# A recurrent transformer kernel on one core: runs written out, the key swap ahead of the feed-forward's wait, and 87 of 361 stages at other steps

## The chip, the cores and the metric

The kernel runs on one core of one Trainium2 chip. A time is the device time of one execution in microseconds. The kernel before takes 2809.85 us, the median of three runs (2808.43 to 2814.73). Durations in this document come from one execution that was also profiled and took 2810.37 us.

The names of the engines in the rows are PE (TensorE, matrix multiply; PEld is its weight load), ACT (ScalarE), DVE (VectorE), POOL (GpSimd) and SP (SyncE, which here only issues transfers; SPq is its queue).

## The reference

```python
for l in range(6):                                   # layers; x is (4, 128, 128)
    x = attention(x, None, ..., causal=True, bias, freqs) + x      # self: 16 heads, one shared key/value head of 64
    x = attention(x, context, ..., causal=False) + x               # cross: context is (4, 2048, 128)
    x = feedforward(x, ...) + x                                    # 128 -> 2*512 gated -> 128
out = layernorm(x, final_g, stable=True) @ proj_w
# attention: layernorm, q = xn@wq, k,v = kv@wkv, one learned null key/value in front,
#            l2norm of q and k, softmax(q k^T + bias), @ v, @ wo, layernorm
# then: x = x + out;  x = x + small 16-head causal attention(layernorm(x));
#       x = x + gated recurrent scan over the batch rows, and a tanh output, of layernorm(x)
```

The bulk is cross attention: for each of 24 pairs of layer and batch row, 16 heads of 128 queries against 2048 keys.

## The kernel before

One **run** is one pair of layer and batch row, n = 0 to 23 (`n // 4` is the layer). The work of a run is in three parts. The **front** (stages whose name begins with `f_`) is self attention, the cross query, and keys and values of the context. The **core** is cross attention. The **back** (`b_`) is the output projection and the feed-forward. Stages of the core outside its tile steps are `e_`; `s_` is setup; `t0_`, `t1_`, `u_`, `v_` are the final tail for batch rows 0, 1, 2 and 3.

The core is cut into 64 tiles (4 groups of 4 heads, 16 blocks of 128 keys), each 128 keys by 512 query columns. A tile is: two float16 score matmuls into one of three PSUM banks `psS` (L1050); ACT takes the exponent twice, once rounded to the matmul's format as `PH` (L885) and once exact as `P` (L888); DVE subtracts, `PL = P - PH` (L634); PE multiplies values with `PH` twice (L1098, L1099) and with `PL` once (L1101), into `psO`. There are 4 buffers for `P` and 8 for `PH` and `PL`. PE runs the value matmuls of a tile 6 steps behind its scores (AHEAD), DVE the subtraction one step behind.

A **window** is 65 steps (one for the null key, then 64 tiles). In one window PE, ACT, DVE and POOL each work on the core of run n, on the front of run n + 1 and on the back of run n - 1. Each engine has a table, PLAN_PE and so on, that names which stages it executes behind its part of step s. An engine executes its instructions in this order and waits at semaphores; nothing else sets the order. So a stage that stands early in an engine's table and waits for another engine holds up every tile step behind it.

Windows 1 to 22 are in a hardware loop of 11 iterations with two windows each (`Fori`, L321); window 0, window 23 and the last one, without a core, are written out. SP has a queue of its own with a loop over layers (L383): `context` loads the context of a run, `swap` (L377, L378) copies the two halves of the keys `KT` onto each other's partitions, and `query_weights`, `front_weights`, `back_weights` load the weights of a layer. The back weights of a layer may be overwritten only when the feed-forward of the last run of the layer before is done (`ff_w2`). PE begins a window by waiting for the swap of that run (`kv_swap`).

Stages that matter below: on PE `f_turn_q_sa` (L1043, turns the self-attention queries), `b_turn` (L1035 on `psA`, turns the normalised row of the back), `f_sk2` (L1050 on `psL`), `f_wo` (L1155 on `psL`), `b_down` (L1213). On DVE `f_unit_sa` (L576), `f_null` (L650 to L652), `f_V3` (L684, L686), `b_out` (L707 and the layernorm behind it, to L491 on `back_xn`), `b_end` (L721). On ACT `f_hi_sa` (L894, L895); on POOL `f_low_sa` (L461 on `qs_all`), `f_klow` (L461 on `ks`) and `f_rot` (L452 to L455).

Of the kernel before, what the change touches and what calls it, by code (L numbers as in the profile page):

```python
# [20 lines left out]
L, B, N, D = 6, 4, 128, 128  # L21
# [11 lines left out]
RUNS = L * B  # L33
# [29 lines left out]
def build(nc, x, ctxT, wpack, gcols, gout, null_k, null_v, tail_w, tail_cols, bo, emb,  # L63
          c_pack, out):
    with ExitStack() as ctx:
# [176 lines left out]
        def at(s, core, back):  # L242
# [8 lines left out]
            0: ["s_bias"], 4: ["f_turn_sa"], 5: ["f_proj_sa", "f_proj_sa2", "f_kv0"], 7: ["f_kv1"], 8: ["u_turn_fin"],  # L251
# [14 lines left out]
            4: ["f_raw_sa", "f_raw_sa2"], 7: ["f_kraw0"], 8: ["f_sq_sa"], 10: ["f_kraw1", "s_table"],  # L266
            13: ["f_hi_sa", "f_kraw2"], 14: ["f_kraw3"], 15: ["f_ksq"], 17: ["f_QT_sa"], 20: ["b_tanh"],
# [3 lines left out]
            41: ["t1_back0"], 45: ["t1_back2"], 52: ["f_raw_ca"], 53: ["f_sq_ca"], 54: ["f_KT"], 59: ["f_hi_ca"],  # L271
            62: ["f_QT_ca"], 65: ["v_gates2", "v_exp0", "v_exp1", "v_exp2", "v_exp3", "v_back0", "v_back2", "v_gates3"],
        }
        PLAN_DVE = {
            0: ["f_begin", "f_norm_sa"], 1: ["e_null", "s_bias", "f_xnT_sa"], 2: ["s_null"], 3: ["b_spread3"],
            4: ["b_invert3"], 5: ["b_widen3"], 6: ["f_V0", "f_V1"], 7: ["b_scale3", "t0_largest", "u_largest"],
            9: ["f_ss_sa", "t0_final", "u_final"], 10: ["s_turned", "s_table"], 11: ["f_V2", "f_unit_sa", "t0_in"],
# [16 lines left out]
            61: ["t1_z"], 64: ["b_end", "u_z"],  # L294
# [3 lines left out]
            0: ["f_sa", "s_null"], 1: ["f_rot"], 6: ["f_sa_q"], 7: ["f_low_sa", "t0_fin", "u_fin", "s_mask"], 11: ["t0_y"],  # L298
            12: ["u_y", "t0_y2", "b_out"], 13: ["b_ff", "f_kv"], 14: ["u_y2"], 16: ["t1_fin"], 19: ["f_klow"], 20: ["t1_y"],
            21: ["t1_y2"], 30: ["f_out"], 37: ["f_ca"], 38: ["s_rows"], 40: ["f_ca_q"], 49: ["f_low_ca"], 54: ["t0_z"],  # L300
            56: ["t1_z"], 60: ["u_z"], 65: ["v_fin", "v_y", "v_y2", "v_z"],
        }

        def drive(eng, plan, stages, core_step=None):
# [16 lines left out]
            with eng.Fori(0, (RUNS - 2) // 2) as k:  # L321
                window((k * 2 + 1, 1), (k * 2, 0), (k * 2 + 2, 0))
                window((k * 2 + 2, 0), (k * 2 + 1, 1), (k * 2 + 3, 1))
# [8 lines left out]
        def _(sp):  # L332
# [50 lines left out]
            with sp.Fori(1, L) as l:  # L383
                context(l * B)
                swap(l * B - 1, 1)
                sp.wait_ge(sem("ca_proj"), l * B * 2)
                query_weights(l)
                front_weights(l)
                context(l * B + 1)
                swap(l * B, 0)  # L390
                context(l * B + 2)
                sp.wait_ge(sem("ff_w2"), l * B)
                back_weights(l)
                swap(l * B + 1, 1)
                context(l * B + 3)
                swap(l * B + 2, 0)
# [1004 lines left out]
```

## Time and profile before

| | |
|---|---|
| median of three runs | 2809.85 us |
| the profiled execution | 2810.37 us, its span from first to last instruction 2808.6 us |
| PE busy | 2519.6 us, 90% |
| DVE busy | 2314.1 us, 82% |
| ACT busy | 2057.7 us, 73% |
| POOL busy | 613.8 us, 22% |
| mean granted clock of TensorE | 0.971 of full |
| first window's first instruction of the core | 97.80 us |
| windows 1 to 22 (the loop) | 197.04 to 2586.13 us |

A busy share is the time in which at least one instruction of the engine is under way. In square brackets behind a row of the timeline stands how long the engine had been idle before that instruction and what released it; "issue" there means that the profile shows nothing that it waited for. DMA transfers are of this kind.

### The profile page before, as it was taken

The page shows a single profiled execution, that of the slowest core. Times are in us where ns is not written, and L with a number is a line of the kernel's source. Part 1 is how long each engine was busy: PE and PEld are TensorE (multiplying, and loading weights), DVE is VectorE, ACT ScalarE, POOL GpSimd, SP SyncE. Part 2 cuts the span into 40 slices and gives each one's busy share as a digit, 9 for nine tenths or more (in the row PEclk, how much of TensorE's full clock was granted, in tenths as well). Part 3 has the DMA queues.
Part 4 walks back from the last instruction along what each step waited for, and adds up shares of the span by engine and source line. Part 5 has one row for each costly group of instructions (what it writes and reads, how often), then busy time and mean ns, then how long its engine had stood idle before and what let it go on. Part 6 is the DMA issues. An engine that isn't in the chain of part 4 may idle for free.

```text
span 2808.6 us, 44144 instructions
## 1 busy us (share of the span) xinstructions
PE 2519.6 (90%) x12652; PEld 1529.2 (54%) x12652; DVE 2314.1 (82%) x4427; ACT 2057.7 (73%) x3861; POOL 613.8 (22%) x392
## 2 busy tenths in 40 slices
PE   4799999989999998999998999998999999999776
PEld 2455555555555555555555555555555555555455
DVE  6688889888888887888887887887888887888876
ACT  2677877777877877778777877877787787788541
POOL 2312312312212213123123123122132131230000
PEclk7899999999999999999999999999999999999986
DMA  3000010000000001001001001001001001000000
GB/s 120 23 8 16 24 34 16 23 29 16 23 31 20 24 1 44 9 16 49 9 16 44 8 16 49 8 16 44 4 21 39 12 23 29 16 9 24 1 1 4
DMA packets 16661, 64.43 MB, mean 23 GB/s; under 512 B 2241, under 2 KB 7410, under 8 KB 11642
## 3 DMA queue, kind: packets, MB, share of 16 engines
q1 hardware_dynamic: 16378, 61.13, 6.8%
q8 instruction: 120, 1.97, 0.3%
q14 instruction: 163, 1.34, 0.1%
HBM read 48.25 MB, written 0.29 MB: 17 GB/s over the span
## 4 chain that ended last, share of the span: by engine, by line
DVE 32%; PE 28%; issue 21%; POOL 10%; ACT 7%; DMA 2%; DVEq 1%; SPq 0%; ACTq 0%; POOLq 0%
DVE PL L634 11%; POOL rn L420 7%; PE psS L1050 6%; PE psO L1098 4%; PE psO L1101 4%; PE psO L1099 4%; DVE rows_sb L613 3%; ACT P L888 3%; DVE rows_sb L605 3%; DVE oTs L618 2%; ACT PH L885 2%; DVE ss L568 2%; PE psL L1155 2%; POOL qs_all L461 2%; PE psL L1162 2%
## 5 line engine op out<-in xcount | busy, mean ns | idle before, releaser
L634 DVE TENSOR_TENSOR PL<-P,PH 128x512 fp32r<-128x512 f32 x1536 | 1126.4, 761 | 121.9 <-ACT P L888 67.9
L885 ACT ACTIVATE PH<-psS 128x512 fp32r<-128x512 f32 x1536 | 955.4, 622 | 155.7 <-PE psS L1050 134.2
L888 ACT ACTIVATE P<-psS 128x512 f32<-128x512 f32 x1536 | 964.2, 628 | 72.8 <-DVE PL L634 72.6
L1050 PE MATMUL psS<-QT,KT 128*128 128x512 f16 x3072 | 926.1, 385 | 0.8 <-ACT P L888 0.7
L1098 PE MATMUL psO<-PH,V 128*128 128x512 f32 x1536 | 880.7, 573 | 0.0
L1101 PE MATMUL psO<-PL,V 128*128 128x512 f32 x1536 | 608.3, 396 | 0.0
L1099 PE MATMUL psO<-PH,VL 128*64 128x512 f32 x1536 | 607.1, 395 | 0.0
L1050 PEld LDWEIGHTS psS<-QT,KT 128*128 128x128 f16 x3072 | 215.1, 99 | 339.5 <-issue 247.0
L1098 PEld LDWEIGHTS psO<-PH,V 128*128 128x128 f32 x1536 | 293.5, 191 | 181.3 <-issue 8.8
L1101 PEld LDWEIGHTS psO<-PL,V 128*128 128x128 f32 x1536 | 289.7, 189 | 154.1 <-issue 2.6
L420 POOL TENSOR_TENSOR rn<-ssc,neghalf 128x16 f32<-128x16 f32 (+2 forms) x73 | 235.6, 3228 | 354.2 <-DVE ssc L569 302.2
L420 POOL TENSOR_TENSOR front_rstd<-front_ve,neghalf 128x1 f32<-128x1 f32 x80 | 43.1, 539 | 1119.0 <-DVE front_ve L489 1119.0
L1099 PEld LDWEIGHTS psO<-PH,VL 128*64 128x64 f32 x1536 | 211.3, 138 | 41.6
L936 ACT ACTIVATE Ps<-psL 128x512 f32<-128x512 f32 x96 | 57.3, 597 | 154.2 <-PE psL L1050 154.2
L461 POOL TENSOR_TENSOR qs_all<-qsq,qs_all 128x1088 f16<-128x1088 f32 (+1 forms) x48 | 116.5, 2427 | 134.4 <-ACT qs_all L895 134.4
L613 DVE STREAM_TRANSPOSE rows_sb<-rcol 64x512 f32<-64x512 f32 x192 | 133.5, 704 | 5.3
L1176 PEld LDWEIGHTS psL<-W,ctx_sb 128*128 128x128 f32 x768 | 99.4, 192 | 23.3 <-ACT qraw L907 14.4
L1043 PE MATMUL psL<-ident,qs_all 128*128 128x128 f16 x768 | 52.2, 222 | 66.4 <-POOL qs_all L461 66.4
L907 ACT ACTIVATE qraw<-psL 128x512 f32<-128x512 f32 x96 | 57.3, 597 | 71.8 <-PE psL L1162 51.8
L1176 PE MATMUL psL<-W,ctx_sb 128*128 128x128 f32 x768 | 104.2, 279 | 1.1 <-ACT kraw L950 1.1
L1144 PE MATMUL psL<-Ps,Vs 128*128 128x512 f32 x192 | 101.5, 611 | 3.4 <-DVE Ps L670 3.4
L461 POOL TENSOR_TENSOR ks<-ksq,ks 128x1024 f16<-128x1024 f32 x24 | 58.6, 2441 | 204.2 <-ACT ks L960 204.2
(365 smaller groups left out, 2844.2 us busy)
## 6 DMA issues: line engine op xcount, KB each, us to landing
ctx_sb<-ctxT SPq DMA_DIRECT2D x24, 1024.0 KB, 4.8
KT<-KT SPq DMA_DIRECT2D x48, 256.0 KB, 3.7
W<-wpack SPq DMA_DIRECT2D x6, 1280.0 KB, 6.3
W<-wpack SPq DMA_DIRECT2D x6, 1088.0 KB, 7.0
W<-wpack SPq DMA_DIRECT2D x6, 576.0 KB, 5.2
KT<-biasM SPq DMA_DIRECT2D x1, 1024.0 KB
W<-tail_w SPq DMA_DIRECT2D x1, 832.0 KB
P<-biasW SPq DMA_DIRECT2D x1, 512.0 KB
```

The costliest lines, as they stand in the source:

```text
L420: nc.gpsimd.tensor_tensor(out_, in_, neghalf[0:out_.shape[0], 0:width], ALU.pow).then_inc(sem(done), 1)
L461: nc.gpsimd.tensor_tensor(half, whole, high, ALU.subtract).then_inc(sem(tag + "_lo"), 1)
L613: nc_v.transpose(rr, rc.unsqueeze(2).broadcast_to([64, QCOL // 32, 32])).then_inc(sem(tag + "_row"), 1)
L634: nc_v.tensor_tensor(PL[:, here, :], P[:, t % PSLOTS, :], PH[:, here, :], ALU.subtract).then_inc(sem("p_lo"), 1)
L885: nc_a.activation(PH[:, t % HSLOTS, :], bank, ACT.Exp, scale=SIM_SCALE).then_inc(sem("p_hi"), 1)
L888: nc_a.activation(P[:, t % PSLOTS, :], bank, ACT.Exp, scale=SIM_SCALE).then_inc(sem("ca_exp"), 1)
L1050: ins = mm(bank, keys[part], q, start=(part == 0), stop=(part == 1))
L1098: mm(bank, V[:, par, j, :], PH[:, here, :], start=False, stop=False)
L1099: mm(bank[0:DH, :], VL[:, par, j, :], PH[:, here, :], start=False, stop=False)
L1101: mm(bank, V[:, par, j, :], PL[:, here, :], start=False, stop=(j == KT_N - 1)).then_inc(sem("ca_pv"), 1)
L1144: mm(psL[:, g % 2, :], Vs[:], Ps[:, g % 2, :], start=True, stop=False)
L1176: ins = mm(psL[:, t % 2, a * 128:(a + 1) * 128], ctx_sb[:, k * 128:(k + 1) * 128], weights(W_CAKV, W_CAKV + 128), start=True, stop=True)
```

## The change

It has three parts. The two hardware loops (all engines' over windows, SP's over layers) become Python loops, so the instructions of every window are written out and the run's number is a constant. On SP, the swap of run 4l + 1 goes ahead of the wait for `ff_w2` and of the load of the back weights. And of the 361 entries in the four tables 87 stand at another step; the tile steps themselves and the stages are unchanged.

```diff
-            with eng.Fori(0, (RUNS - 2) // 2) as k:
+            for k in range((RUNS - 2) // 2):
                 window((k * 2 + 1, 1), (k * 2, 0), (k * 2 + 2, 0))
                 window((k * 2 + 2, 0), (k * 2 + 1, 1), (k * 2 + 3, 1))
...
-            with sp.Fori(1, L) as l:
+            for l in range(1, L):
                 context(l * B)
                 swap(l * B - 1, 1)
                 sp.wait_ge(sem("ca_proj"), l * B * 2)
...
                 context(l * B + 2)
+                swap(l * B + 1, 1)
                 sp.wait_ge(sem("ff_w2"), l * B)
                 back_weights(l)
-                swap(l * B + 1, 1)
                 context(l * B + 3)
                 swap(l * B + 2, 0)
...
-            15: ["u_turn_y2", "t0_turn_y2"], 16: ["f_turn_q_sa", "t0_qkv"], 18: ["b_turn", "u_qkv"],
+            14: ["b_wo"], 15: ["u_turn_y2", "t0_turn_y2"], 16: ["t0_qkv"], 18: ["f_turn_q_sa", "b_turn", "u_qkv"],
```

Moved on PE among others: `f_turn_sa` 4 to 2, `f_proj_sa` 5 to 3, `f_kv0` stays at 5, `f_turn_q_sa` 16 to 18, `f_sk2` 32 to 33, `f_sv0` 26 to 25, `f_sv2` 38 to 36, `f_turn_k` 53 to 55, `f_turn_q_ca` 62 to 63, `b_down` 59 to 64. On DVE: `f_null` 17 to 13, `b_out` 14 to 13, `f_spread0` 27 to 24, `f_scale0` 31 to 29, `f_scale3` 46 to 45, `f_out` 48 to 47.

On PE, in the part of a window with the self queries (`qs_all`, 16 transposes) and the back's row (`back_xn`). Before, in the loop:

```order
L1043 MATMUL psL<-ident,qs_all 128x128 x16
L1076 REGISTER_ALU
L1050 MATMUL psS<-QT,KT 128x512 x2
L1098 MATMUL psO<-PH,V 128x512
L1099 MATMUL psO<-PH,VL 64x512
L1101 MATMUL psO<-PL,V 128x512
L1076 REGISTER_ALU
L1050 MATMUL psS<-QT,KT 128x512 x2
L1098 MATMUL psO<-PH,V 128x512
L1099 MATMUL psO<-PH,VL 64x512
L1101 MATMUL psO<-PL,V 128x512
L1035 MATMUL psA<-C,back_xn 128x128
```

The same place on PE after the change (line numbers are two higher, and the register instructions of the loop are gone):

```order
L1052 MATMUL psS<-QT,KT 128x512 x2
L1100 MATMUL psO<-PH,V 128x512
L1101 MATMUL psO<-PH,VL 64x512
L1103 MATMUL psO<-PL,V 128x512
L1045 MATMUL psL<-ident,qs_all 128x128 x16
L1037 MATMUL psA<-C,back_xn 128x128
L1052 MATMUL psS<-QT,KT 128x512 x2
```

The two tile steps that stood between the turned queries and the back's row stand ahead of both.

On DVE, the stretch from the last subtraction ahead of `b_out` (`back_x` is its first tile, `PL` a tile's subtraction). Before:

```order
L634 TENSOR_TENSOR PL<-P,PH 128x512
L707 ISA
L707 TENSOR_SCALAR back_x<-xs 128x128
L60 ISA
L486 BN_STATS back_stats<-psA 128x6
L60 REGISTER_ALU
L487 MEMSET back_fence 1x1
```

After the change, from `f_unit_sa` (`qsq`) on:

```order
L578 TENSOR_TENSOR qsq<-qraw,rn 128x1088
L636 TENSOR_TENSOR PL<-P,PH 128x512 x2
L652 TENSOR_SCALAR nkcs<-NKC 128x64
L653 TENSOR_SCALAR nkc<-NKC 128x64
L654 TENSOR_TENSOR nvs<-NVH,own_group 128x4x64
L686 CAST V<-psL 128x4x64
L688 TENSOR_TENSOR VL<-psL,V 128x256
L709 TENSOR_SCALAR back_x<-xs 128x128
L488 BN_STATS back_stats<-psA 128x6
```

The three instructions of `f_null` and the two of `f_V3` now stand directly ahead of `b_out`, where a subtraction stood.

On SP, the transfers around the load of the back weights. Before:

```order
L371 DMA ctx_sb<-ctxT 128x2048
L345 ISA
L345 DMA W<-wpack 128x2560
L346 ISA
L346 DMA gca<-gout 128x128
L377 DMA KT<-KT 64x2048
L378 DMA KT<-KT 64x2048
L370 ISA
L371 DMA ctx_sb<-ctxT 128x2048
```

After:

```order
L373 DMA ctx_sb<-ctxT 128x2048
L379 DMA KT<-KT 64x2048
L380 DMA KT<-KT 64x2048
L347 DMA W<-wpack 128x2560
L348 DMA gca<-gout 128x128
L373 DMA ctx_sb<-ctxT 128x2048
```

The two halves of the swap stand ahead of the weights, and ahead of the wait that belongs to them.

## Rows read from the trace of the kernel before

**Rows 1.** Windows: us, busy us of PE, PEld, DVE, ACT, POOL, clock, DMA, GB/s.

```profile
411.89:518.55 106.66, 100.27 (x513) 60.62 (x513) 90.72 (x169) 83.88 (x158) 25.05 (x15) 1.00 0.05 16
...
738.52:847.05 108.53, 100.25 (x514) 60.60 (x514) 92.56 (x173) 85.62 (x161) 25.06 (x15) 1.00 0.10 32
...
953.71:1065.19 111.48, 100.24 (x513) 60.61 (x514) 93.03 (x174) 85.62 (x161) 25.05 (x15) 1.00 0.09 28
1065.19:1174.61 109.42, 102.96 (x514) 61.65 (x514) 90.34 (x169) 83.86 (x158) 25.08 (x15) 0.97 0.05 15
...
97.80:197.04 99.24, 93.20 (x455) 52.88 (x455) 82.75 (x141) 82.37 (x157) 22.59 (x12) 0.98 0.05 17
```

**Rows 2.** Timeline, PE: the first matmuls of windows 1, 9, 11 and 23.

```profile
197.04 0.61 PE L1057 MATMUL psS<-QT,nkc 128*32 128x512 f16 x8 [0.28 <-ACT P L888]
...
1065.19 1.04 PE L1057 MATMUL psS<-QT,nkc 128*32 128x512 f16 x8 [5.08 <-issue]
...
1283.18 0.61 PE L1057 MATMUL psS<-QT,nkc 128*32 128x512 f16 x8 [2.22 <-ACT P L888]
...
2586.13 0.61 PE L1057 MATMUL psS<-QT,nkc 128*32 128x512 f16 x8 [0.38 <-ACT P L888]
```

**Rows 3.** Timeline, DVE: the first subtraction of windows 11 and 23.

```profile
1285.69 0.69 DVE L634 TENSOR_TENSOR PL<-P,PH 128x512 fp32r<-128x512 f32 x1 [3.50 <-issue]
...
2587.25 0.69 DVE L634 TENSOR_TENSOR PL<-P,PH 128x512 fp32r<-128x512 f32 x1 [0.28 <-DVE xs L721]
```

**Rows 4.** Timeline, SP's queue: transfers ahead of window 9, and of window 11.

```profile
1053.31 0.35 SPq L345 DMA_DIRECT2D W<-wpack  x1
...
1054.28 0.47 SPq L377 DMA_DIRECT2D KT<-KT  x1
...
1270.46 0.47 SPq L377 DMA_DIRECT2D KT<-KT  x1
```

**Rows 5.** DMA issues: count, KB each, median us from issue to landing.

```profile
KT<-KT SPq DMA_DIRECT2D x48, 256.0 KB, 3.7
W<-wpack SPq DMA_DIRECT2D x6, 1280.0 KB, 6.3
```

**Rows 6.** Stretches around the start of window 9, columns as in rows 1.

```profile
1060.00:1065.00 5.00, 0.10 (x1) 0.00 (x0) 1.20 (x3) 1.32 (x3) 0.00 (x0) 0.93 0.27 63
1065.00:1068.50 3.50, 3.31 (x14) 1.40 (x15) 2.24 (x8) 1.08 (x2) 0.54 (x1) 0.50 0.02 7
```

**Rows 7.** Timeline, PE: the four long waits inside window 12 (from 1389.85).

```profile
1418.48 1.05 PE L1043 MATMUL psL<-ident,qs_all 128*128 128x128 f16 x16 [1.86 <-POOL qs_all L461]
...
1423.27 0.33 PE L1035 MATMUL psA<-C,back_xn 128*128 128x128 f32 x1 [1.47 <-DVE back_xn L491]
...
1446.33 0.60 PE L1050 MATMUL psL<-QTs,KTs 128*128 128x512 f16 x2 [1.01 <-DVE oTs L618]
...
1470.24 2.05 PE L1155 MATMUL psL<-W,oTs 128*128 128x128 f32 x16 [1.26 <-DVE oTs L618]
```

**Rows 8.** Timeline, window 12: the chain on DVE, ACT and POOL ahead of those waits.

```profile
1412.94 1.29 DVE L576 TENSOR_TENSOR qsq<-qraw,rn 128x1088 f32<-128x1088 f32 x1 [1.56 <-POOL rn L420]
...
1414.42 1.09 ACT L895 ACTIVATE qs_all<-qsq 128x1088 f16<-128x1088 f32 x1
...
1415.60 2.73 POOL L461 TENSOR_TENSOR qs_all<-qsq,qs_all 128x1088 f16<-128x1088 f32 x1 [2.69 <-ACT qs_all L895]
...
1416.14 2.74 DVE L634 TENSOR_TENSOR PL<-P,PH 128x512 fp32r<-128x512 f32 x1
...
1418.80 0.22 DVE L707 TENSOR_SCALAR back_x<-xs 128x128 f32 x1
```

**Rows 9.** All subtractions of the run: duration ns min/median/max.

```profile
L634 DVE TENSOR_TENSOR PL<-P,PH x1536: 674/691/2741, 102.5 to 2708.3; 128x512 fp32r<-128x512 f32 x192
```

**Rows 10.** Timeline, the last window: `b_down` on PE, `b_end` on DVE.

```profile
2755.00 1.92 PE L1213 MATMUL psA<-W,hu 128*128 128x128 f32 x8
...
2757.44 0.28 DVE L721 TENSOR_TENSOR xs<-back_x,psA 128x128 f32<-128x128 f32 x1
```

More of the change, by code:

```diff
@@ L250, in build @@
         PLAN_PE = {
-            0: ["s_bias"], 4: ["f_turn_sa"], 5: ["f_proj_sa", "f_proj_sa2", "f_kv0"], 7: ["f_kv1"], 8: ["u_turn_fin"],
[11 rows of a table removed]
+            0: ["s_bias"], 2: ["f_turn_sa"], 3: ["f_proj_sa", "f_proj_sa2"], 5: ["f_kv0"], 6: ["f_kv1", "s_null"],
+            8: ["u_turn_fin"], 10: ["s_table"], 11: ["t0_turn_fin", "u_proj"], 12: ["f_kv2"], 13: ["f_kv3", "t0_proj"],
+            14: ["b_wo"], 15: ["u_turn_y2", "t0_turn_y2"], 16: ["t0_qkv"], 18: ["f_turn_q_sa", "b_turn", "u_qkv"],
+            20: ["t1_turn_fin", "f_turn_k_sa", "b_gate", "f_sn"], 21: ["t0_s0"],
[8 rows of a table added]
+            63: ["f_turn_q_ca", "t1_turn_z"], 64: ["b_down"],
             65: ["v_turn_fin", "v_proj", "v_turn_y2", "v_qkv", "v_gates2", "v_s0", "v_s1", "v_s2", "v_s3", "v_turn0", "v_turn1", "v_turn2", "v_turn3", "v_pv0", "v_pv1", "v_pv2", "v_pv3", "v_turn_o", "v_wo", "v_turn_z", "v_gates3"],
@@ L265, in build @@
         PLAN_ACT = {
-            4: ["f_raw_sa", "f_raw_sa2"], 7: ["f_kraw0"], 8: ["f_sq_sa"], 10: ["f_kraw1", "s_table"],
-            13: ["f_hi_sa", "f_kraw2"], 14: ["f_kraw3"], 15: ["f_ksq"], 17: ["f_QT_sa"], 20: ["b_tanh"],
[3 rows of a table removed]
-            41: ["t1_back0"], 45: ["t1_back2"], 52: ["f_raw_ca"], 53: ["f_sq_ca"], 54: ["f_KT"], 59: ["f_hi_ca"],
-            62: ["f_QT_ca"], 65: ["v_gates2", "v_exp0", "v_exp1", "v_exp2", "v_exp3", "v_back0", "v_back2", "v_gates3"],
+            2: ["f_raw_sa"], 3: ["f_raw_sa2"], 7: ["f_kraw0"], 8: ["f_sq_sa"], 9: ["s_table", "f_kraw1"], 12: ["f_kraw2"],
+            13: ["f_hi_sa"], 15: ["f_kraw3"], 16: ["f_ksq"], 17: ["f_QT_sa"], 20: ["f_sne"], 21: ["b_tanh"],
[4 rows of a table added]
+            59: ["f_hi_ca"], 63: ["f_QT_ca"],
+            65: ["v_gates2", "v_exp0", "v_exp1", "v_exp2", "v_exp3", "v_back0", "v_back2", "v_gates3"],
         }
         PLAN_DVE = {
-            0: ["f_begin", "f_norm_sa"], 1: ["e_null", "s_bias", "f_xnT_sa"], 2: ["s_null"], 3: ["b_spread3"],
-            4: ["b_invert3"], 5: ["b_widen3"], 6: ["f_V0", "f_V1"], 7: ["b_scale3", "t0_largest", "u_largest"],
-            9: ["f_ss_sa", "t0_final", "u_final"], 10: ["s_turned", "s_table"], 11: ["f_V2", "f_unit_sa", "t0_in"],
[16 rows of a table removed]
-            61: ["t1_z"], 64: ["b_end", "u_z"],
+            0: ["s_bias", "f_begin", "f_norm_sa", "f_xnT_sa"], 1: ["e_null"], 2: ["s_null"],
+            5: ["b_spread3", "b_invert3", "b_widen3", "f_V0"], 6: ["f_V1"], 7: ["t0_largest", "u_largest"], 8: ["f_ss_sa"],
+            9: ["t0_final", "u_final", "b_scale3"], 10: ["s_turned", "s_table"], 11: ["f_V2", "f_unit_sa", "t0_in"],
+            12: ["u_in"], 13: ["f_null", "f_V3", "t0_norm", "b_out", "t0_gain"], 14: ["u_norm"],
[13 rows of a table added]
+            48: ["t0_res", "f_xnT_ca"], 50: ["u_out", "s_rows"], 51: ["t0_z"], 54: ["e_spread2", "f_ss_ca"],
+            55: ["e_invert2", "e_widen2"], 56: ["f_KT"], 57: ["f_unit_ca", "u_cols", "t1_out"], 59: ["t1_cols", "t1_res"],
+            60: ["e_scale2", "u_res"], 61: ["f_nv", "t1_z"], 64: ["b_end", "u_z"],
             65: ["v_largest", "v_final", "v_in", "v_norm", "v_gain", "v_own", "v_key0", "v_key1", "v_cell2", "v_mask0", "v_key2", "v_mask1", "v_key3", "v_mask2", "v_sum0", "v_mask3", "v_sum1", "v_sum2", "v_sum3", "v_back1", "v_back3", "v_out", "v_cols", "v_res", "v_z", "v_cell3"],
@@ L297, in build @@
         PLAN_POOL = {
[L298 to L301, printed above, removed]
+            0: ["f_sa"], 1: ["s_null"], 5: ["f_rot", "f_sa_q"], 7: ["t0_fin", "u_fin"], 8: ["s_mask"], 9: ["f_low_sa"],
+            11: ["t0_y"], 12: ["u_y", "t0_y2", "b_out"], 13: ["b_ff"], 14: ["u_y2", "f_kv"], 16: ["t1_fin"], 20: ["t1_y"],
+            21: ["t1_y2"], 23: ["f_klow"], 26: ["f_out"], 35: ["f_ca"], 38: ["s_rows"], 40: ["f_ca_q"], 48: ["f_low_ca"],
+            54: ["t0_z"], 56: ["t1_z"], 60: ["u_z"], 65: ["v_fin", "v_y", "v_y2", "v_z"],
         }
```

54 rows, old and new, of tables (PLAN_ACT, PLAN_DVE, PLAN_PE) are left out of this document.

## The prediction, made before the changed kernel had run

> **What bounds the kernel now.** I read four views: the busy shares, the stretches by window, the timeline of PE at the window starts, and the timelines of PE, DVE, ACT and POOL inside one plain window.
>
> The busy shares say PE at 90%, DVE at 82%. The stretches say more [rows 1]: the plain window 3 lasts 106.66 us with PE busy for 100.27, and a core in which PE never waited would need about 100.3. So each window has 6.4 us that belong to waits of PE inside it, and no other engine is near its own limit (DVE 90.7, ACT 83.9).
>
> The loop's 22 windows run from 197.04 to 2586.13 us [rows 2], 2389.1 us. At 106.66 each they would take 2346.5. The other 42.6 us are of three kinds, and the same rows tell them apart. Which window is which follows from the run number: the loop jumps back after every second window, and a layer's load of weights falls after every fourth.
>
> - Window 6 (108.53 us) ends with a jump and nothing else. The cause is on DVE: its first subtraction after a jump starts after 3.50 us of idle with nothing waited for at 1285.69 [rows 3], while on entering window 23, where no jump is, the same gap is 0.28. PE then finds its first matmul 2.22 us late [rows 2]. Cost 1.6 to 1.9 us, five times: 8.0 (three in ten of DVE's gap is hidden by other slack).
> - Window 8 (111.48 us) ends with a jump and with PE's wait for the swapped keys, 5.08 us [rows 2]. SP's queue shows the reason: the load of the back weights goes out at 1053.31, the swap at 1054.28, so both sat behind the wait for `ff_w2`, of a `b_down` that stands at step 59 of 65; at window 11 the swap went out at 1270.46, 12.7 us ahead of the window [rows 4]. Cost 111.48 − 106.66 = 4.8, five times, with the other four like it: 23.5.
> - Window 9 (109.42 us) follows such a wait. Its mean clock is 0.97 and PE is busy for 102.96 us in place of 100.27 [rows 1]; after the 5 us without a matmul the granted clock is 0.50, which is 1.2 GHz, for the first 3.5 us, where it had been 0.93 during the idle slice [rows 6]. Cost about 2.2, five times: 11.0.
>
> 8.0 + 23.5 + 11.0 = 42.5, the excess to within 0.1.
>
> **Part one, the loops written out.** It removes the jump, and the register instructions (two rows of the order printed above are such). The latter cost nothing to be seen: window 0, written out already, is 99.24 us with PE busy 93.20 [rows 1], so PE is idle for 6.0 us there and for 6.4 in the loop. It adds code. Window 0 again is the row for its price: no stretch of it shows a gap without a cause, so I take zero for straight code, with at most a few us in all kept in the range. DVE's gap after the jump goes in all ten places.
>
> The Trainium skill, page "Runtime: NRT & Kernel Launch", section "Instruction fetch mechanics", says that instructions are fetched ahead in sequence only, that a taken branch to a block not at hand must fetch before it goes on, and that passing from block to block in straight code is mostly hidden. The trace agrees in the two places it can speak: 3.50 against 0.28 us.
>
> **Part two, the swap ahead of the `ff_w2` wait.** It now waits only for its own keys. Those are made at steps 55 and 56, so it can go out some 92 us into a window of about 104; a swap takes 3.7 us from issue to landing [rows 5]. It lands 8 us before it is wanted. What stands behind it in SP's queue is the load of `W`, 1280 KB and 6.3 us [rows 5]. The load waits for `b_down`, now at step 64, so it lands some 6 us into the next window. Its first reader is `b_wo` at step 14, about 22 us in: 15 us to spare. The next context load is issued behind it, for a use far off. So the 5.08 us wait goes whole, and with it the slow stretch behind it. Together with part one: −42.6 us. (With the swap alone moved the jump would still cost its 1.6 in those five windows.)
>
> **Part three, the tables.** Here the waits inside the window are priced. Window 12 has four long ones [rows 7]: 1.86 for `qs_all`, 1.47 for `back_xn`, 1.01 and 1.26 for `oTs`; small ones (0.2 to 0.3 each) make up the 6.4.
>
> The first two. PE stood ready for the queries at 1418.48 − 1.86 = 1416.62, that is 26.8 us into the window. Now two tile steps stand ahead of them, 2.3 us (a step is 1.15 us: 1.05 us of transposes and two steps lie between the 1418.48 and the 1421.80 at which PE was ready for `back_xn`). So PE comes to them at about 29. POOL's `f_low_sa`, which it waits for, ran from 1415.60, or 25.8 us in, for 2.73 us [rows 8]. Its chain begins at L576, which had waited 1.56 us for POOL's `rn`; `f_ss_sa` ahead of it is a step earlier now, so I move the chain up by 1.3: POOL works from 24.4 to about 26.6 or 27.1. The wait of 1.86 is gone.
>
> Then `back_xn`. It was finished at 1423.27, 4.4 us behind the first instruction of `b_out`, `back_x` at 1418.80 [rows 8]. That one started late since the subtraction ahead of it, 1416.14, took 2.74 us. The median of all 1536 is 0.69, the longest 2.741 [rows 9]. It began while POOL's two-input operation ran and ended with it: DVE was held. Which instruction is held in the new order? `f_null` and `f_V3` stand ahead of `b_out` in step 13. The first has `nvs`, with both inputs in SBUF like the subtraction, and DVE comes to it at about 24.5, just when POOL begins. If it is held until 26.6, `b_out` begins at 27.9 and `back_xn` comes at 32.3, against 33.4 before: PE waits some 2.5 us there, and 1.1 of the 3.33 us of the two waits is won. If `nvs` slips in ahead of POOL it comes at 31.7 (1.7 won); if neither is held, at 30.2, and all is won.
>
> The Trainium skill, page "SBUF — State Buffer", section "Who interferes with whom", gives the hold as a rule: the port pair that VectorE and GpSimd share is an exclusive lock for the whole instruction, and a VectorE operation with two SBUF inputs contends for it with a GpSimd operation that reads SBUF. The 2.74 us beside 0.69 agrees. It speaks against this change, for it also covers `nvs`; by it the low figure, 1.1, would stand.
>
> The others. `f_sk2` goes from step 32 to 33 with its key work on DVE and ACT about where it was: its 1.01 goes. `f_wo` stays at 48 while `f_scale3` and `f_out` come one step up: I take 0.9 in place of 1.26, since the group before it (`e_scale1` now at 47) eats part. Against this, `f_klow` on POOL (now step 23) holds a subtraction about 0.5 us, and `f_sv3` at 42 comes two steps behind `f_sp3` (now 40) in place of four: I take 0.85 us of new wait. Net +0.1 to +0.3 of gain.
>
> Per window this gives 1.3 (all held), 2.0 (`nvs` first), 3.5 (nothing held); never over 6.4, and below nothing only if a new hold reaches PE. I take **2.0**, the middle of what the hold can do, as it depends on 0.1 us which of the two comes first: 22 × 2.0 = 44.
>
> **The ends.** Window 0: −1, by the same tables. In the last window `b_down` was at 2755.00, 1.92 us long, and `b_end` 0.5 us behind its end [rows 10]; now it stands behind all of the window's other work on PE, on the way to the tail: +2.5, up to +4. The prologue (`s_bias` first on DVE): ±1.
>
> **Sum**, against the profiled 2810.4 (median of the runs 2809.85, so 0.5 less): 2810.4 − 42.6 − 44 − 1 + 2.5 = 2725.3. The kernel's measurement can tell about 0.2%, or 5.6 us.
>
> **Rivals.**
>
> A. *The moves take nearly all waits.* Holds land on subtractions with slack behind them (six steps of AHEAD on PE, 6.9 us, hide a late `PL`). For: most of what DVE does in a window is not awaited at once by PE. Against: `back_xn` has no slack. 5.5 us a window: 2810.4 − 42.6 − 121 − 1 + 2.5 = 2648.
>
> B. *The moves give nothing.* Each wait taken away turns up at the next stage: PE reaches `b_turn` a microsecond sooner and waits there, and `f_wo` and `f_sv3` likewise. For: the DVE chain of `b_out` (4.4 us) is unchanged, and DVE is busy for 90.7 of 106.7. Then only part one and two count: 2768.
>
> C. *Slower.* VectorE is held by GpSimd once or twice more per window at a place PE waits for: `nvs` by `f_low_sa`, `back_x` by `b_out`'s own operation on POOL, both ahead of `b_turn`. A hold costs up to 2.74 − 0.69 = 2.05 us. Against: today's hold is at the same place, so it is replaced, not added. Beyond 42.6 / 22 = 1.9 us a window it makes the kernel slower; with +3.5, two such holds less one wait: 2845.
>
> D. *The change does not do what it says.* Straight code on five engines stalls for fetches about as much as the jumps did, and the tables give little: 2790 to 2815. Against: window 0.
>
> **How the numbers follow.** Forecast (2697 to 2747) 0.50; A 0.24; B 0.17; C 0.05; D 0.04, half of it within 0.2%. The range takes the forecast's case, B's 2768, and A down to 2660: 2660 to 2768. Faster 0.50 + 0.24 + 0.17 + 0.02 = 0.93; same 0.02; slower 0.05.
>
> **What would show it.** Right: no first matmul of a window waits over 0.5 us, DVE has no 3 us gap without a cause, the mean clock is above 0.98, windows 1 to 22 are alike at about 104.6 us, PE waits for `back_xn` 2 to 3 us and no more for `qs_all`, and `nvs` is long. Wrong: a wait at window starts (the swap or `W` late), PE gaps "issue" at regular distances (fetches), or a window at 101 us (A) or 106.6 (B); B would show the old sum of waits under other names.

## The result, and the profile after

The changed kernel takes 2606.53 us (median of four runs, 2605.07 to 2613.90) against 2811.64 for the kernel before on the same chip: a ratio of 0.9276, 95% interval 0.9255 to 0.9297. The forecast was 2725 with a range of 2660 to 2768. The sign was right; the gain is 205 us where 85 were forecast, and the time lies below the range.

The stretches of the profiled execution (2605.6 us span) by window. The columns are start:end, length, busy us of PE, PEld, DVE, ACT and POOL with instruction counts, granted clock, DMA share, GB/s. These are windows 6, 8, 9 and 0, four of the five of [rows 1].

```profile
687.87:787.73 99.86, 99.18 (x512) 60.65 (x512) 88.35 (x172) 84.03 (x160) 24.62 (x15) 1.00 0.11 34
887.60:987.46 99.86, 99.18 (x514) 60.66 (x514) 88.34 (x172) 84.03 (x160) 24.61 (x15) 1.00 0.06 17
987.46:1087.32 99.86, 99.18 (x512) 60.64 (x512) 88.34 (x172) 84.03 (x160) 24.60 (x15) 1.00 0.09 31
94.66:188.56 93.90, 92.59 (x453) 53.43 (x453) 80.65 (x142) 82.10 (x157) 23.33 (x12) 0.97 0.06 18
```

The kinds of window of [rows 1] are gone: windows 1 to 22 are all 99.84 to 99.87 us, and these have the clock at 1.00. PE is idle for 0.68 us in each, where it was 6.4. The timeline of PE at the starts of windows 9 and 11, places of [rows 2]: no wait stands behind the rows. The same holds for the others, but for window 1, whose first matmul waits 0.94 us.

```profile
987.46 0.61 PE L1059 MATMUL psS<-QT,nkc 128*32 128x512 f16 x8
...
1187.18 0.61 PE L1059 MATMUL psS<-QT,nkc 128*32 128x512 f16 x8
```

SP's queue ahead of window 9, the place of [rows 4]. The swap goes out at 978.54, 8.9 us ahead of the window's start, and the load of `W` behind it at the boundary:

```profile
978.54 0.46 SPq L379 DMA_DIRECT2D KT<-KT  x1
...
987.44 0.33 SPq L347 DMA_DIRECT2D W<-wpack  x1
```

Window 12 begins at 1287.04. Of the four long waits of [rows 7] and the small ones beside them, the list of PE's waits in it (total us, times, longest) has one left:

```profile
PE psA L1037 <- DVE back_xn L493: 0.6, 1, 0.6
```

The chain ahead of it, on DVE and on POOL, which answers to [rows 8]:

```profile
1308.11 1.29 DVE L578 TENSOR_TENSOR qsq<-qraw,rn 128x1088 f32<-128x1088 f32 x1
1309.32 1.29 DVE L636 TENSOR_TENSOR PL<-P,PH 128x512 fp32r<-128x512 f32 x2
...
1310.72 0.42 DVE L654 TENSOR_TENSOR nvs<-NVH,own_group 128x256 fp32r<-128x256 f32 x1
1311.06 0.42 DVE L686 CAST V<-psL 128x256 fp32r<-128x256 f32 x1
1311.51 0.42 DVE L688 TENSOR_TENSOR VL<-psL,V 128x256 fp32r<-128x256 f32 x1
1311.85 1.50 DVE L709 TENSOR_SCALAR back_x<-xs 128x128 f32<-128x128 f32 x1
```

```profile
1310.77 2.50 POOL L463 TENSOR_TENSOR qs_all<-qsq,qs_all 128x1088 f16<-128x1088 f32 x1 [2.69 <-ACT qs_all L897]
1314.16 0.54 POOL L422 TENSOR_TENSOR back_rstd<-back_ve,neghalf 128x1 f32<-128x1 f32 x1 [0.90 <-DVE back_ve L491]
```

`nvs` begins 0.05 us before POOL's operation and takes its usual 0.42 us, in this window as in all the others. The two instructions of `f_V3` read PSUM and pass at 0.42 each while POOL works. `back_x`, 0.22 us long in [rows 8], takes 1.50 and ends at 1313.35, just behind POOL's 1313.27. POOL seems to be held in its turn: its operation takes 2.26 us where no two-input instruction of DVE runs across its start (e4_null_late, below), 2.45 and 2.50 where `nvs` runs 0.33 and 0.38 us into it (e9_row_early, and here), and 2.73 in [rows 8], where a subtraction ran 0.62 us into it. On PE the two stages that now stand together:

```profile
1315.93 1.07 PE L1045 MATMUL psL<-ident,qs_all 128*128 128x128 f16 x16
1317.60 0.33 PE L1037 MATMUL psA<-C,back_xn 128*128 128x128 f32 x1 [0.60 <-DVE back_xn L493]
```

Where the 203 us between the two profiled spans lie, with e1_loops_swap (parts one and two alone, below) between them:

| stretch, us | before | e1_loops_swap | after |
|---|---|---|---|
| to the first matmul of window 0 | 97.80 | 96.70 | 94.66 |
| window 0 | 99.24 | 99.34 | 93.90 |
| windows 1 to 22 | 2389.1 | 2342.6 | 2197.3 |
| window 23 to the end | 222.5 | 224.4 | 219.8 |

### The profile page after: what moved, and what is told of

It is laid out like the page before. It is cut to its first block, busy times and chain, and to the rows that moved or that the text cites. A ratio compares the mean times of both kernels' runs of the same rounds, so it can differ in the third digit from the quotient of the medians.

```text
span 2605.6 us, 37962 instructions
## 1 busy us (share of the span) xinstructions
PE 2482.2 (95%) x12652; PEld 1522.6 (58%) x12652; DVE 2238.7 (86%) x4427; ACT 2042.3 (78%) x3861; POOL 604.8 (23%) x392
## 4 chain that ended last, share of the span: by engine, by line
PE 58%; DVE 17%; ACT 13%; issue 8%; POOL 3%; DMA 0%; SPq 0%; ACTq 0%; DVEq 0%; POOLq 0%
PE psS L1052 16%; PE psO L1100 9%; PE psO L1101 9%; PE psO L1103 9%; ACT P L890 6%; ACT PH L887 5%; DVE PL L636 4%; PE psL L1146 3%; PE psL L1157 2%; PE psL L1052 2%; DVE back_x L709 1%; ACT qraw L909 1%; POOL back_rstd L422 1%; DVE V L686 1%; PE psA L1203 1%
## 5 line engine op out<-in xcount | busy, mean ns | idle before, releaser
L887 ACT ACTIVATE PH<-psS 128x512 fp32r<-128x512 f32 x1536 | 1009.4, 657 | 177.3 <-PE psS L1052 158.7
L636 DVE TENSOR_TENSOR PL<-P,PH 128x512 fp32r<-128x512 f32 x1536 | 1038.5, 711 | 94.5 <-ACT P L890 84.6
L890 ACT ACTIVATE P<-psS 128x512 f32<-128x512 f32 x1536 | 1009.3, 657 | 108.5 <-DVE PL L636 108.3
L938 ACT ACTIVATE Ps<-psL 128x512 f32<-128x512 f32 x96 | 66.8, 696 | 39.1 <-PE psL L1052 37.7
L463 POOL TENSOR_TENSOR ks<-ksq,ks 128x1024 f16<-128x1024 f32 x24 | 51.5, 2145 | 171.9 <-ACT ks L962 171.9
L620 DVE TENSOR_TENSOR oTs<-psL,rows_sb 64x256 f32<-64x256 f32 x192 | 80.2, 418 | 6.1
L620 DVE TENSOR_TENSOR oT<-psO,rows_sb 64x256 f32<-64x256 f32 x192 | 80.2, 418 | 6.1
```

What stands on the lines that cost most here:

```text
L463: nc.gpsimd.tensor_tensor(half, whole, high, ALU.subtract).then_inc(sem(tag + "_lo"), 1)
L620: nc_v.tensor_tensor(dst[64 * odd:64 * odd + 64, 2 * g:2 * g + 2, :], bank[0:64, :].rearrange("p (c a n) -> p c a n", a=2, n=N)[:, :, odd, :],
L636: nc_v.tensor_tensor(PL[:, here, :], P[:, t % PSLOTS, :], PH[:, here, :], ALU.subtract).then_inc(sem("p_lo"), 1)
L887: nc_a.activation(PH[:, t % HSLOTS, :], bank, ACT.Exp, scale=SIM_SCALE).then_inc(sem("p_hi"), 1)
L890: nc_a.activation(P[:, t % PSLOTS, :], bank, ACT.Exp, scale=SIM_SCALE).then_inc(sem("ca_exp"), 1)
```

## The experiments

Each is an edit of the changed kernel unless the text says otherwise; times are medians, to be compared with 2606.5 (changed) and about 2811 (before, run with them each time).

**Parts one and two without the tables: e11_swap_only and e1_loops_swap.** The edits to the kernel before are the SP hunk of the diff alone, and that with both loops written out.

> The kernel before with part two alone: the swap ahead of the ff_w2 wait, loops and tables as before. By the prediction's sizes: five waits of 4.8 us become plain jumps of 1.6 and the five slow stretches (2.2 us each) go, 26.5 us less, 2785 (2780 to 2790); so writing the loops out is worth the other 19 of e1_loops_swap's 2765. Rival: the jump covers the same microseconds as the wait, so with the jumps still there little is won, 2800 or more, and the loops are what pays.

> The kernel before with parts one and two alone: loops written out and the swap ahead of the ff_w2 wait, all four tables as before. Theory T1 (the parts add up; the tables took every wait inside the window and were under-sized in the prediction): 42.6 us less than before, 2768 (2763 to 2773), the window 106.7 us, no long first matmul of a window. Theory T2 (writing the loops out is worth more than the jumps, and the tables less): 2740 or less, the window shorter than 105 us.

Measured: the swap alone 2787.78 us, ratio 0.992 (0.9905 to 0.9936); with the loops 2765.35, ratio 0.9837 (0.9821 to 0.9854). So the swap is worth 23 (26.5 expected), the loops another 22 (16), together 46 where the sum had 42.6. All 22 windows of e1_loops_swap but one (106.11) are 106.48 to 106.53 us, one of them here:

```profile
1367.17:1473.65 106.48, 100.28 (x512) 60.61 (x513) 91.44 (x172) 84.72 (x160) 24.71 (x15) 1.00 0.09 29
```

T1 stands and T2 falls: in the old order these two parts are worth what was forecast, and the other 159 us are the tables'.

**The swap put back: e2_swap_behind.**

```diff
+                sp.wait_ge(sem("ff_w2"), l * B)
+                back_weights(l)
                 swap(l * B + 1, 1)
-                sp.wait_ge(sem("ff_w2"), l * B)
-                back_weights(l)
```

> The changed kernel with the swap of run 4l+1 put back behind the ff_w2 wait and the load of the back weights. The changed kernel takes 2606.5. Theory T1 (parts add up with the prediction's sizes): five waits of 4.8 us and five slow stretches of 2.2, +35 us, 2641. Theory T3 (the parts depend on each other: b_down now stands at step 64, so the swap goes out only near the window's end, 10 to 12 us ahead of its landing): five waits of some 11 us, +60 to +75, 2666 to 2681.

Measured 2667.99 us, ratio 0.9489 (0.9473 to 0.9505): +61. T3 stands. The first matmul of window 5 on PE, the swap for it in SP's queue, and windows 4 and 5:

```profile
596.45 1.05 PE L1059 MATMUL psS<-QT,nkc 128*32 128x512 f16 x8 [9.50 <-issue]
```

```profile
587.89 0.47 SPq L379 DMA_DIRECT2D KT<-KT  x1
```

```profile
487.14:596.45 109.31, 99.18 (x512) 60.69 (x513) 90.43 (x179) 84.98 (x161) 25.15 (x16) 0.97 0.09 28
596.45:697.95 101.50, 100.80 (x514) 61.37 (x514) 86.30 (x164) 83.23 (x158) 24.08 (x14) 0.98 0.06 16
```

The swap, which stands behind the wait for `b_down`, goes out 0.9 us after PE was ready for it (596.45 − 9.50 = 586.95). In the kernel before it went out 5.8 us ahead of that moment (1054.28 against 1065.19 − 5.08 = 1060.11, [rows 4] and [rows 2]), as `b_down` stood at step 59 and not 64. So the same two lines cost 61 us here. The 23 us of e11_swap_only are not their cost alone, since five jumps stayed at the same places; the prediction's 23.5 + 11.0 = 34.5 for the waits and the slow stretches is the number to compare. The old tables with the swap behind and the loops written out were not run.

**The loops kept: e3_loops_kept, e10_loops_down59, e12_loop_PE, e13_loop_DVE.** The first two keep `Fori` on all engines and SP, the second with `b_down` at step 59 as well; the others keep it on one engine, PE or DVE (`pair` holds the two windows of a pass):

```diff
+            if plan is PLAN_DVE:
+                with eng.Fori(0, (RUNS - 2) // 2) as k:
+                    pair(k)
+            else:
+                for k in range((RUNS - 2) // 2):
+                    pair(k)
```

> The changed kernel with the two hardware loops kept (ten jumps back). Theory T1: a jump costs what it cost before, 1.6 to 1.9 us, +17 us, 2623. Theory T4 (before, part of DVE's 3.5 us gap was covered by waits that the tables have removed, now all of it reaches PE): 3.5 us a jump, +35, 2641. If PE's lead over DVE covers it: under +8.

> The changed kernel with both hardware loops kept (as in e3_loops_kept, 2671) and b_down back at step 59 on PE. Theory T7 (ten jumps cost 64 us there because b_down is the last thing ahead of the jump: the load of the weights and the last PE work fall on it): 2606 + 20 to 35 = 2626 to 2641. Rival T8 (a jump costs some 6 us wherever no other wait covers it: each engine's own 3 us gap and the slow stretch behind it): 2660 to 2675 as before.

> The changed kernel with a hardware loop on PE alone (ten jumps on PE, none on DVE, ACT, POOL and SP). Theory T8 (each engine's own jump stops it, and PE has nothing to hide it behind now): 3 us a jump and 2 of slow clock behind it, +40 to +55, 2646 to 2661. Rival T9 (what PE loses at a jump is DVE's late first subtraction): under +10, 2616 or less.

> The changed kernel with a hardware loop on DVE alone. Theory T9: +40 or more, 2646 or more. Theory T8: DVE's 3 us gap is covered in part by the buffers between DVE and PE, 0 to 2.5 us reach PE, +0 to +25, 2606 to 2631.

Measured: 2671.07 (all loops), 2663.35 (with `b_down` at 59), 2649.74 (PE's alone), 2665.97 (DVE's alone), ratios to before 0.9504, 0.947, 0.9431 and 0.9487. T1, T4 and T7 fall. T8 has e10_loops_down59 and PE's own jump (+43) right, but DVE's alone costs +59, which is T9's figure; of T9 the other half falls, since PE's jump costs too. DVE's is 6 us a jump on average. Where it goes, on DVE: the first subtraction after the jumps into windows 3 and 5 (in e13_loop_DVE), and then on PE:

```profile
392.50 0.69 DVE L643 TENSOR_TENSOR PL<-P,PH 128x512 fp32r<-128x512 f32 x1 [3.12 <-ACT P L897]
...
598.03 0.69 DVE L643 TENSOR_TENSOR PL<-P,PH 128x512 fp32r<-128x512 f32 x1 [6.44 <-issue]
```

```profile
395.12 0.33 PE L1044 MATMUL psL<-C,front_xn 128*128 128x128 f32 x1 [2.21 <-DVE front_xn L500]
...
600.65 0.47 PE L1044 MATMUL psL<-C,front_xn 128*128 128x128 f32 x1 [5.53 <-DVE front_xn L500]
```

PE waits in `f_turn_sa`, at step 2 now (step 4 before). And at 598 the gap is twice as long. In SP's queue of the same run the weights were on their way:

```profile
591.30 0.33 SPq L354 DMA_DIRECT2D W<-wpack  x1
```

That load (1280 KB) was issued 0.3 us before DVE's gap began (598.03 − 6.44 = 591.59). The profile also shows the packets with which instructions are fetched, in queues of their own. The DMA queues in 390.4:390.9, 591.6:596.0 and 596.0:596.1 (packets, MB, share of the 16 engines):

```profile
q14 instruction: 1, 0.01, 4.3%
...
q1 hardware_dynamic: 132, 1.28, 83.4%
...
q1 hardware_dynamic: 22, 0.02, 52.8%
q14 instruction: 1, 0.01, 19.3%
```

At the plain jump an instruction packet comes 1.4 us into the window, at this one 4.7 us in, when the load is nearly through. It is so in all five windows of either kind, and the changed kernel, which has no jump, has no such packet at these places. So the longer gap is a fetch that comes late, behind the load. The windows with the longer gap (107.7 to 108.1 us in place of 102.2 to 103.7) are 5, 9, 13, 17 and 21, those with this load; the windows behind such a jump also lose clock (0.97 in this one):

```profile
591.31:699.09 107.78, 101.62 (x512) 61.87 (x512) 88.57 (x172) 84.03 (x160) 24.90 (x15) 0.97 0.09 28
```

The Trainium skill, page "Runtime: NRT & Kernel Launch", section "Instruction fetch mechanics", says that a sequencer fetches its instructions through a DMA queue of its own, and that a taken branch whose target is not at hand stops it until the target has been fetched. The trace agrees: 3.1 us of gap where only an instruction packet moves in it, 6.4 with the load ahead of that packet.

On PE's own jump (e12_loop_PE) the load does not add: the first matmul waits 3.0 to 4.1 us after the five plain jumps and 1.8 to 2.3 after the five with the load, which goes out there about when PE's gap begins. What sets these gaps was not looked into further.

**Whether the place of `f_turn_sa` covers the jump: e15_loop_DVE_turn4 and e18_turn4.** PE's `f_turn_sa` goes to step 4, `f_proj_sa` and `f_proj_sa2` to 5, ACT's `f_raw_sa` and `f_raw_sa2` to 4, with and without DVE's loop.

> e13_loop_DVE with f_turn_sa, f_proj_sa and f_raw_sa back at steps 4 and 5, to be read against e18_turn4, the same without a loop. Cover theory (in the new order PE asks for the front's first row at step 2 and so finds DVE's gap after the jump, in the old one two steps, 2.3 us, later): a jump costs 0 to 3.5 us, 10 to 25 us over e18. Rival (the place of f_turn_sa does not matter to the jump): 50 to 60 us over e18, as e13 over the changed kernel.

> The changed kernel with f_turn_sa, f_proj_sa and f_raw_sa back at steps 4 and 5 (all loops written out). The chain qraw, rn, qs_all starts 2.3 us later: if it is what ends last ahead of b_turn, PE's wait there grows by 1.5 to 2.3 us a window and the time by 33 to 50, 2640 to 2657; if the chain has slack, 2606.

Measured: 2638.65 with the loop, 2610.86 without, a difference of 28 where it was 59 (the 22 windows alone: 29.6 and 53.6). The windows behind the five plain jumps are 100.1 us, 0.1 more than the others of that run; those behind a jump with the load are 103.5 to 105.8. So the cover theory holds, a little above its figure. e18_turn4's windows are 99.83 to 99.86 us, and its 4 us over the changed kernel lie behind window 22: that chain has slack, and the two steps earlier for `f_turn_sa` are worth nothing in the windows of a kernel without loops.

**What one hold costs: e4_null_late and e9_row_early.**

```diff
-            12: ["u_in"], 13: ["f_null", "f_V3", "t0_norm", "b_out", "t0_gain"], 14: ["u_norm"],
+            12: ["u_in"], 13: ["f_V3", "f_null", "t0_norm", "b_out", "t0_gain"], 14: ["u_norm"],
```

```diff
-            9: [...], 11: ["f_V2", "f_unit_sa", "t0_in"],
+            9: [...], 11: ["b_x", "f_V2", "f_unit_sa", "t0_in"],
...
-            def b_out(n, par):
+            def b_x(n, par):
                 begin("back", n, BACK_LINKS)
                 link = links["back"]
                 link(nc_v.tensor_scalar(back.x, xs[:, n % B, :], 1.0, None, ALU.mult))
+
+            def b_out(n, par):
+                link = links["back"]
```

> The changed kernel with f_V3 ahead of f_null in step 13 on DVE. In the changed kernel nvs starts 0.05 us ahead of POOL's 2.50 us f_low_sa and is not held (0.42 us in all 24 windows), while back_x is (1.50 us). Hold theory: f_null's three instructions now start while POOL's operation runs, at least nvs is held until it ends, back_x comes some 0.6 to 0.8 us later than now and PE's wait for back_xn grows from 0.6 to 1.2 or 1.4: +13 to +18 us, 2620 to 2625. Rival (the order inside the step is nothing, b_out waits for POOL in any case): 2606, within 3 us.

> The changed kernel with b_out's first instruction (back_x, a copy of a row of the residual, which POOL's f_low_sa holds for 1.3 us) moved to the head of step 11 on DVE, ahead of f_unit_sa. Hold theory: nothing in front of the row's statistics is held; back_rstd on POOL then waits for the end of f_low_sa instead, and back_xn comes 0.7 to 0.9 us earlier; the last wait of a window (0.60 us) is gone: window 99.2 to 99.3, 13 us less than the changed kernel, 2593 (2590 to 2597). Rival (the hold moves on to the next instruction of the kind, back_ve, and the chain is as late as now): 2606, within 3 us.

Measured: e4_null_late 2618.54 us, ratio 0.9315 (0.93 to 0.9331), 12 us more. Its window is 100.16 and PE's wait for `back_xn` 0.9 us. DVE in step 13 of window 12, and POOL:

```profile
1315.40 1.77 DVE L652 TENSOR_SCALAR nkcs<-NKC 128x64 f16<-128x64 f16 x1
...
1317.19 0.41 DVE L654 TENSOR_TENSOR nvs<-NVH,own_group 128x256 fp32r<-128x256 f32 x1
1317.53 0.21 DVE L709 TENSOR_SCALAR back_x<-xs 128x128 f32<-128x128 f32 x1
```

```profile
1314.86 2.26 POOL L463 TENSOR_TENSOR qs_all<-qsq,qs_all 128x1088 f16<-128x1088 f32 x1 [2.69 <-ACT qs_all L897]
```

The hold is there, on `nkcs` and not on `nvs`, and it costs 0.3 us a window, not the 0.6 to 0.8 expected: whichever is first of the kind bears it, and the rest of `f_null`, 0.4 us, comes behind instead of ahead. That is 6.8 of the 12 us over windows 1 to 22; the rest is in the stretches before and behind them.

e9_row_early 2593.36 us, ratio 0.9221 (0.9205 to 0.9236). This is the fastest kernel of the study, 13 us below the changed one, as the hold theory said. Its windows are 99.12 us, 0.74 less (16 us in the 22); the end took 3.0 us more in the profiled execution. `back_x` takes 0.22 us at 1299.78, POOL's operation runs from 1303.53 to 1305.98 with no instruction of that kind behind it on DVE, and PE has no wait left:

```profile
1303.44 0.41 DVE L654 TENSOR_TENSOR nvs<-NVH,own_group 128x256 fp32r<-128x256 f32 x1
1305.11 0.15 DVE L491 TENSOR_SCALAR back_ve<-back_mv 128x1 f32<-128x1 f32 x1
1306.51 0.41 DVE L493 TENSOR_SCALAR back_xn<-psA,back_mv,back_rstd 128x128 f32<-128x128 f32 x1 [1.25 <-POOL back_rstd L422]
```

```profile
1279.57:1378.67 99.10, 99.01 (x512) 60.66 (x512) 87.04 (x172) 84.03 (x160) 24.53 (x15) 1.00 0.06 17
```

The Trainium skill, page "SBUF — State Buffer", section "Who interferes with whom", lists `tensor_scalar` among the VectorE operations that can take the port pair shared with GpSimd, on conditions for its operands. The trace agrees for `back_x` (1.50 beside 0.22 us) and `nkcs` (1.77 beside 0.19); the one-column `back_ve` was not held (0.15 us in the middle of POOL's operation).

**The tables cut in two: e7_early_new and e8_late_new; then by engine: e16_late_DVE and e17_late_PE.** "Early" are the stages that stand at step 19 or earlier in either kernel. A stage has its new step and its place in the list from the changed kernel, or both from the kernel before.

> The changed kernel with new steps only for stages that stand at step 19 or earlier (in either kernel), old steps for all later ones. Theory T5 (each half of the tables removes its own waits): the wait for qs_all is gone and that for back_xn about 0.6 us, the later waits of the kernel before (1.01 at f_sk2, 1.26 at f_wo, 0.2 to 0.4 of small ones) stay, so the window is 99.9 + 2.7 = 102.6 to 103.3 us, the time 2606 + 60 to 75 = 2666 to 2681. Rival T6 (a wait removed early only comes back at the next late stage, so only both halves together pay): window 105.5 or more, 2730 or more.

> The changed kernel with old steps for stages at step 19 or earlier (in either kernel), new ones for all later. Theory T5: the two early waits of the kernel before (1.86 and 1.47 us) stay, the late ones are gone: window 99.9 + 2.9 to 3.7 = 102.8 to 103.5, 2606 + 65 to 90 = 2671 to 2696 (with window 0 and the prologue a few us more). Rival T6: 2730 or more.

> e7_early_new (2704.7, window 103.85) with DVE's late steps new as well, those of PE, ACT and POOL old. Theory T10 (the late waits are PE waiting for oTs, which DVE's moves bring 1 to 4 us earlier): window 100.9 or less, 2640 or less. Rival T11 (PE's own order, with f_sv0 and f_sv2 earlier and f_sk2 later, takes them away): 103 or more, 2685 or more.

> e7_early_new with PE's late steps new as well, those of DVE, ACT and POOL old. Theory T10: window 103 or more, 2685 or more, with waits for oTs and Ps at other lines. Rival T11: window 101 or less, 2645 or less.

| kernel | early steps | late steps | us | plain window, us |
|---|---|---|---|---|
| e1_loops_swap | old | old | 2765.35 | 106.5 |
| e8_late_new | old | new | 2751.23 | 105.4 |
| e7_early_new | new | old | 2704.68 | 103.9 |
| e16_late_DVE | new | new on DVE alone | 2759.01 | 106.4 |
| e17_late_PE | new | new on PE alone | 2750.39 | 105.2 |
| the changed kernel | new | new | 2606.53 | 99.9 |

(Ratios to before 0.9782, 0.9618, 0.9814 and 0.9784 for the four between, each within 0.0023.) Early alone brings 61, late alone 14, both 159: 84 us belong to neither. Each theory misses at least one of its two runs. T5 misses both, T6 has only e8_late_new right, T11 only e16_late_DVE and T10 only e17_late_PE. With the new early steps, moving the late stages of DVE alone costs 54 us and those of PE alone 46, and together (with ACT and POOL) they bring 98. PE's waits in window 12 of e7_early_new, then of e16_late_DVE and e17_late_PE, the largest of each:

```profile
PE psL L1162 <- DVE oTs L625: 1.2, 1, 1.2
PE psL L1057 <- DVE oTs L625: 0.9, 1, 0.9
PE psS L1064 <- ACT P L895: 0.8, 2, 0.4
```

```profile
PE psL L1058 <- DVE oTs L626: 1.0, 1, 1.0
PE psO L1109 <- DVE PL L642: 0.9, 1, 0.9
PE psL L1152 <- DVE Ps L678: 0.8, 2, 0.6
```

```profile
PE psL L1161 <- DVE oTs L624: 2.1, 1, 2.1
PE psL L1056 <- ACT hu L951: 0.8, 1, 0.8
```

In e8_late_new the cut made a wait of its own (PE's `f_sk0` moved up to step 22, DVE's `f_KT_sa` left at 21), so its 14 us understate the late half:

```profile
PE psL L1057 <- DVE KTs L671: 2.4, 1, 2.4
```

Seven of its windows are also 1.2 to 1.6 us longer than the rest, at a mean clock of 0.98. By an estimate from these rows the wait is worth 22 × 2.4 = 53 us and the slow stretches 10 of the 84. Without the wait its window would be 105.4 − 2.4 = 103.0, inside T5's 102.8 to 103.5, so the two halves are nearer to independent than the raw times say. That estimate was not tested. What these runs do show is that a cut through the tables makes new waits: the steps of the four tables fit each other. Which pair of stages would be enough was not tried, and the runs by engine say nothing of what one engine's moves are worth in their own tables.

**`b_down` back at step 59 on top of the fastest: e14_row_down59.**

> e9_row_early (2593.4) with b_down back at step 59 on PE. By the prediction's term for the end, b_down at step 64 lies on the way to b_end and the tail and costs 2.5 us once: 2591 (2589 to 2592). Rival: b_end's step on DVE (64) sets the end of the window as before, no difference, 2593; or b_down comes ahead of its input and each window waits, 2600 or more.

Measured 2602.32 us, ratio 0.9258 (0.9246 to 0.9271): 9 us more. The rival's "2600 or more" has the number. The stretch from window 23 to the end is 222.3 us against e9_row_early's 222.8, too small a difference to read (see below), but the 2 us of `b_down` are on the chain that ends last in e9_row_early and not here: from its matmul of `qraw` to the copy `W` behind it it takes 2.54 us there (2540.36 to 2542.90) and 0.59 here (2548.08 to 2548.67). Each window is 99.50 in place of 99.12:

```profile
PE psS L1062 <- ACT QT L908: 0.9, 2, 0.5
```

With `b_down` away from step 64, only one tile step stands on PE between `f_turn_q_ca` at 63 and the next window's first matmul, which reads what ACT makes of it. So the move costs 2 us once and covers 0.4 us in each window.

## Why the prediction was wrong

- **Parts one and two** were right: 42.6 us summed, 45.8 measured in the old order, with the waits, gaps and slow stretches gone as named. (A jump cost 1.1 to 1.9 us in the five windows, not 1.6 to 1.9; their sum, 8.0, is right.) That the parts add up was an assumption and is false: next to the new tables the swap's place is worth 61 us and the loops 64. It did no harm only because all three were made together, which is luck and not method.
- **The tables' term is the step that failed**: 2.0 us a window, measured 6.6 (106.5 to 99.86), so 145 us in place of 44. It charged waits that never came and left out a gain in busy time: PE's idle time fell by 5.5 us a window (6.20 to 0.68, from e1_loops_swap to the changed kernel) and its busy time by 1.1 (100.28 to 99.18). Of the working, by its steps:
  - The wait for `qs_all` gone: right. PE came to `f_turn_q_sa` 28.9 us into the window, 29 forecast.
  - The wait for `back_xn`: 2.5 us forecast, 0.60 measured. POOL began at 23.7 us instead of 24.4, as its chain gained 2.0 us and not 1.3; and the held instruction was not `nvs`. It won the race by 0.05 us, and both instructions of `f_V3` ran under POOL's operation. I had put them behind it, which is where most of the 1.7 us between forecast (32.3) and trace (30.6) lie.
  - New waits of 0.9 us at `f_wo` and 0.85 at `f_sv3`: neither exists. In window 12 `oTs` is ready 0.5 us before PE comes to `f_wo`, and group 3's `Ps` 0.8 us before `f_sv3`. These charges came from a walk through the tables.
  - "Never over 6.4": wrong as a bound. It took PE's busy time as fixed at 100.3; busy time itself fell to 99.18 as the waits went (99.80 and 99.99 in e8 and e7, 99.01 in e9_row_early). What makes it fall was not tested.
- **Middle value.** The prediction had nearly no waits as rival A, at 24% and 5.5 us a window. That is what the idle time did; the other 1.1 us are the busy time, which no rival had. Taking 2.0 of 1.3, 2.0 and 3.5 looked at the hold alone and let new waits downstream eat most of the other gains, as in rival B. In the new tables no wait came up there. In e16_late_DVE and e17_late_PE waits did come up under other names, but by cutting the tables apart, and more than rival B has.
- **Window 0 and the prologue** gave 5.3 and 3.1 us, forecast 1 and 0.
- **The end**: `b_down` on the way to the tail was right as a mechanism, at 2.0 us where 2.5 were forecast. The chain that ended last, after the change and then before:

```profile
2554.75 0.48 PE psL L1037
2555.23 1.72 PE psA L1215 x8
2556.97 0.30 DVE xs L723
2557.30 0.29 DVE W L829
```

```profile
2757.58 0.49 PE psL L1035
2758.16 0.29 DVE W L827
```

That is 2.55 us against 0.58 between the same two instructions. Yet the whole stretch from window 23 to the end was 2.7 us shorter. It varies between 219.8 and 226.5 us over the kernels of this study, so that a term of this size can be read from the chain and not from the stretch.
- **The signs named beforehand**: alike windows and no wait for `qs_all` came as said. Not so the clock, 0.976 in the profiled execution and 0.974 to 0.978 in the four, where above 0.98 was named; nor the first matmul of window 1 (0.94 us); nor a long `nvs`.
- **Rival C**, a hold ahead of `b_turn`: the hold is there, on `back_x`, for 1.3 us, and costs 0.74 us a window (e9_row_early). It replaced a longer one.

## What to carry to other kernels

When a kernel's order is one table per engine, price a new set of tables as a whole, and distrust a cut through it: one half of this one brought 61 us, the next share on DVE alone cost 54, the whole brought 159, and part of the difference is waits that the cut itself made. If the bound engine is busy for 94% of a window and no other is over 86%, "no wait is left" is a candidate for the likeliest case, and PE's busy time with its waits is not the floor. For a hold between DVE and POOL look at which instruction starts first and what behind it is not held: a small copy moved out of the way was worth 13 us.

## What was not expected of the hardware

- A jump back stopped DVE for 3.1 us, and for 6.4 when a 1280 KB load had been issued 0.3 us before (e13_loop_DVE); the instruction packet came 1.4 and 4.7 us into the window. What that costs depends on what another engine asks of DVE in the first steps behind it: 2.3 to 3.8 us at a plain jump and 7.8 to 8.2 with the load when PE asks at step 2, 0.1 and 3.5 to 5.8 at step 4 (e15_loop_DVE_turn4). The same load did not lengthen the gap of PE's own jump (e12_loop_PE).
- A PE gap of 3.4 us (e12_loop_PE, first matmul of window 3) was followed by a window at a mean granted clock of 0.98 and 1.6 us more of PE busy time. After gaps of 2.25 and 2.26 us in the same run (windows 5 and 9) the clock was 1.00 once and 0.98 once, so the length of the gap alone does not decide it.
- A GpSimd operation was longer by about what a two-input VectorE instruction that had begun before it still had to run: 2.26, 2.45, 2.50 and 2.73 us with 0, 0.33, 0.38 and 0.62 us of overlap at its start.
- A one-input `tensor_scalar` of 128x128 float32, and one of 128x64 float16, are held by a GpSimd operation like the two-input subtraction; one of 128x1 is not.
